# A two-layer recurrent block on one core: keys and queries of the first attention loaded in the projection's tail, one barrier less at each seam, and two engines' round loops written out

## The chip, the cores and the metric

One Trainium2 chip, of whose cores the kernel uses one. The program is written engine by engine: TensorE (PE, and PEld for its weight loads), VectorE (DVE), ScalarE (ACT), GpSimd (POOL) and SyncE (SP) each have a stream of instructions, and they meet only through semaphores. The metric is the time of one execution in device microseconds; the median over several executions is compared.

## The reference

Two layers. Each normalises x, computes an attention s and a feed-forward value g, and adds s * g to x. Only what the kernel does differently per layer matters here:

```python
x = L0_attn_x                                  # [2, 2048, 256], 16 heads of 16
xn = layernorm(x)
s = L0_attn(xn)                                # full softmax attention over 2048 keys
g = silu(L0_ffn(xn))                           # 8 experts, router softmax, cumulative sum over time
x = x + s * g
xn = layernorm(x)
s = L1_attn(xn)                                # banded attention: |i - j| <= 64
g = silu(L1_ffn(xn))                           # 8 LoRA experts, gate softmax
x = x + s * g
return x

# the first attention
qkv = einsum('bld,ed->ble', x, w_qkv) + b_qkv
attn = softmax(einsum('blhc,bmhc->bhlm', q, k) / sqrt(256))
heads = einsum('bhlm,bmhc->blhc', attn, v).reshape(b, l, d)
return einsum('bld,ed->ble', heads, w_o) + b_o + x
```

## The kernel before

Seven phases follow each other, with their starts in the profile: `phase_weights` (0 us), `phase_project` for layer 0 (44), `phase_attend_full` (213), `phase_combine_experts` (1660), `phase_project` for layer 1 (1971), `phase_attend_band` (2069) and `phase_combine_lora` (2331 to the end). Each opens one `nc.Block` with a program for each engine. A block ends with a barrier of all engines. Each phase takes its tiles and semaphores through an object `Names`; when the phase is over, `Names.release` (L85 to L89) clears the semaphores and has a second barrier of all engines. Buffers that several phases share belong to outer `Names` objects (tags k0 to k3), which release the same way, so at the first attention's start two such barriers stand behind the block's own.

`phase_project` walks over 4 chunks of 512 tokens (i) of 2 batches (u). For each chunk, TensorE makes queries, keys, values and the router's hidden layer, VectorE and ScalarE move them out of PSUM, and SyncE stores them to DRAM: `store_parts` (L476, 4 DMAs of 512 KB: queries and keys, each value split in a high and a low half) and `store_values` (L482, one of 544 KB). SyncE's last steps are the waits for all these stores (L532 to L538). Each DMA of SyncE goes onto one ring, in the order of its program. `load_rows`, `store_xn` and `store_turned` stand on it too. GpSimd computes inverse roots for the layernorm.

`phase_attend_full` works in NIT = 32 rounds: 8 groups of 4 heads, 4 chunks of 512 queries in each. The four heads lie in two slots and two sides of 64 partitions; a side holds three copies of 16 rows, for the high and low halves. Per round there are two passes:

- the maximum pass, NU = 32 units: `maximum_scores` (L1147, two matmuls of 128 queries by 512 keys), then `maximum` on VectorE (L1026) over 1024 columns. `whole_maxima` (L1034) closes it. The maxima are turned by TensorE, split into two halves by VectorE (`split_maxima`), and written by GpSimd as extra rows of the query tile Q (`store_maxima`, L984, 4 small DMAs), where the second score matmul subtracts them.
- the exponential pass, NJ = 43 steps: `scores` (L1173), `exponential` on ScalarE (L1091, up to 1024 columns into the ring `prob`), and `add_values` (L1185), which multiplies with the values V and accumulates in PSUM. `copy_output` (L1098), the turn back and `normalise` give `o_out`, which GpSimd stores (`store_output`, L990).

The passes are interleaved: while round r is exponentiated, the maxima of round r + 1 are taken. Before the first round there is a prologue of 32 units without exponentials. In it TensorE also turns eight weight tiles (`turn_weights`, L1240), in units 1 to 8. Ahead of all that, VectorE clears `ps_o` (L1059) and runs the router's softmax (`router_weights_vector`, L1815 to L1831) with ScalarE's exponential (L1805) between L1817 and L1819.

What the first units need comes by DMA at the start of the phase. SyncE issues 12 key loads of slot 0 and slot 1 (`load_first_keys`, L818, 128 KB each into 16 partitions), 18 query loads (`load_first_queries`, L827, 64 KB each), then four loads of V (`load_v`, L944), then, when all keys and queries have landed, the 30 loads of group 1 (`load_halves`, L795 and L799). ScalarE issues the six loads of the first queries itself, and four loads of rows of ones. TensorE waits for them at L1247 to L1256. GpSimd's program ends with a wait for all output stores (`pool.wait_ge(o_stored, ...)`); in `phase_attend_band` SyncE ends with such a wait.

The rounds of TensorE, VectorE, ScalarE and GpSimd are loops (`Fori`) over two rounds each; VectorE's loop spans rounds 0 to 29, ScalarE's rounds 1 to 30, while round 0 of ScalarE is written out.

## Time and profile before

| | us |
|---|---|
| median of 3 runs | 2436.63 |
| lowest and highest | 2425.33, 2439.51 |
| profiled execution | 2435.27 |
| its span | 2433.4 |
| mean granted TensorE clock | 0.956 |
| share of the span busy: PE, DVE, ACT | 91%, 76%, 59% |

The runs are whole executions; the profiled one is a single execution, and its span runs from the first instruction to the last. All rows below have their times in microseconds from the start of that span. A row of the timeline gives start, duration, engine, source line, operation and tiles; "SPq" and the like is an engine's instruction queue, where semaphore and DMA-issuing instructions stand. The landing time of a DMA is counted from its issue. "PEclk" is the granted clock as a share of full speed, "DMA" the mean busy share of the 16 DMA engines. In the view of busy time by stretch the columns are the stretch, its length, the busy time (and number of instructions) of PE, PEld, DVE, ACT and POOL, PEclk, the DMA share, and GB/s.

### The profile page before, as it was taken

What the parts mean: (1) busy time and instruction counts of PE and PEld (TensorE: products, weight loads), DVE (VectorE), ACT (ScalarE), POOL (GpSimd) and SP (SyncE); (2) the same over time, 40 slices, a digit from 0 to 9 for tenths busy, and PEclk for the clock granted to TensorE, in tenths of its full rate; (3) what the DMA queues carried; (4) which work ended last, traced back from release to release, by engine and by line L of the source; (5) the groups of instructions that cost most, each with busy time, mean ns of one, the idle gap of its engine ahead of it and who ended that gap; (6) DMA issues with size and microseconds to landing.
All of it is one profiled execution on the core that took longest, in us unless ns stands there. A gap on an engine that the chain in (4) does not pass through costs nothing. (4 is left out here: it accounts for less than half of the span.)

```text
span 2433.4 us, 43647 instructions
## 1 busy us (share of the span) xinstructions
PE 2212.6 (91%) x14912; PEld 1228.7 (50%) x14912; DVE 1839.2 (76%) x3240; ACT 1442.7 (59%) x2160; POOL 462.6 (19%) x673
## 2 busy tenths in 40 slices
PE   7896899999999999999999999988999987899988
PEld 4664333333333333333333333326888876666678
DVE  5664999999999999999999999912444466888745
ACT  3443377777777777777777777772222222366743
POOL 0000000000000000000000000003545520366745
PEclk9997699999999999999999999989999999688999
DMA  6888400500500501403205002006576459766664
GB/s 206 283 288 183 53 6 6 62 6 8 62 3 13 57 3 26 44 6 44 26 3 64 6 8 62 3 3 176 154 186 157 135 190 373 170 145 146 154 164 130
DMA packets 189129, 231.90 MB, mean 95 GB/s; under 512 B 72720, under 2 KB 122768, under 8 KB 186064
## 3 DMA queue, kind: packets, MB, share of 16 engines
q1 hardware_dynamic: 176048, 210.46, 35.3%
q10 hardware_dynamic: 7184, 14.10, 2.7%
q0 software_dynamic: 5728, 5.00, 0.9%
q8 instruction: 117, 1.92, 0.4%
q14 instruction: 52, 0.43, 0.1%
HBM read 138.97 MB, written 89.13 MB: 94 GB/s over the span
## 5 line engine op out<-in xcount | busy, mean ns | idle before, releaser
L1026 DVE TENSOR_REDUCE a_maxes<-a_ps_a 128x2 f32<-128x1024 f32 x1024 | 1202.2, 1221 | 114.3 <-PE a_ps_a L1147 110.5
L1091 ACT ACTIVATE a_prob<-a_ps_s 128x512 f32<-128x512 f32 (+1 forms) x1376 | 1035.7, 804 | 355.2 <-PE a_ps_s L1173 349.5
L1173 PE MATMUL a_ps_s<-a_Q,a_K 50*128 50x512 f32 x2048 | 596.3, 455 | 89.8 <-ACT a_prob L1091 89.6
L1147 PE MATMUL a_ps_a<-a_K,a_Q 48*128 48x512 f32 x2048 | 551.9, 455 | 26.0 <-DMA a_Q<-s_halves 14.4
L1185 PE MATMUL a_ps_o<-a_prob,a_V 128*17 128x512 f32 x4096 | 544.9, 604 | 0.1
L1173 PEld LDWEIGHTS a_ps_s<-a_Q,a_K 50*128 50x128 f32 x2048 | 278.4, 186 | 508.7 <-ACT a_prob L1091 459.7
L1147 PEld LDWEIGHTS a_ps_a<-a_K,a_Q 48*128 48x128 f32 x2048 | 245.8, 189 | 231.5 <-issue 107.9
L984 POOL DMA_DIRECT2D a_Q<-a_m_parts x128 | 64.3, 503 | 1286.9 <-DVE a_m_parts L1018 1280.3
L1593 DVE CUSTOM_DVE_ANT_0 a_scratch<-a_ps_a,k_mask 128x256 f32<-128x256 f32 (+1 forms) x512 | 178.0, 411 | 25.9 <-PE a_ps_a L1710 24.0
L1653 ACT ACTIVATE a_prob<-a_ps_s 128x512 f32<-128x512 f32 (+1 forms) x256 | 135.6, 583 | 98.8 <-PE a_ps_s L1746 97.3
L1185 PEld LDWEIGHTS a_ps_o<-a_prob,a_V 128*17 128x17 f32 x4096 | 68.0, 95 | 150.9 <-issue 99.0
L1710 PE MATMUL a_ps_a<-k_K,k_Q 48*128 48x256 f32 (+1 forms) x512 | 120.4, 359 | 16.3 <-PEq L89 11.5
L1746 PE MATMUL a_ps_s<-k_Q,k_K 50*128 50x256 f32 (+2 forms) x576 | 105.8, 314 | 12.6 <-DMA k_K<-k_ones 7.0
L1572 POOL TENSOR_SCALAR_AFFINE_SELECT a_prob<-a_prob 128x512 f32<-128x512 f32 (+1 forms) x128 | 79.5, 621 | 130.0 <-ACT a_prob L1653 129.0
L1746 PEld LDWEIGHTS a_ps_s<-k_Q,k_K 50*128 50x128 f32 x576 | 80.2, 203 | 42.3 <-ACT a_prob L1653 16.7
L2122 POOL TENSOR_TENSOR c_pT<-c_wp,c_pT 128x512 fp32r<-128x512 f32 x64 | 82.9, 1295 | 94.8 <-ACT c_pT L2045 94.8
L1710 PEld LDWEIGHTS a_ps_a<-k_K,k_Q 48*128 48x128 f32 x512 | 83.7, 217 | 27.6 <-issue 11.9
L2045 ACT ACTIVATE c_pT<-c_wp 128x512 fp32r<-128x512 f32 x64 | 40.5, 633 | 93.6 <-DVE c_wp L2086 89.6
L2019 PE MATMUL c_ps_g<-k_UO,c_pT 128*128 128x256 f32 x768 | 94.8, 280 | 0.0
L2019 PEld LDWEIGHTS c_ps_g<-k_UO,c_pT 128*128 128x128 f32 x768 | 92.9, 188 | 0.0
L2159 DVE TENSOR_TENSOR c_sums<-c_ps_s,c_sums 128x256 f32<-128x256 f32 x32 | 13.6, 424 | 90.2 <-ACT c_th L2056 90.2
L1575 POOL TENSOR_SCALAR_AFFINE_SELECT a_prob<-a_prob 128x512 f32<-128x512 f32 (+1 forms) x128 | 79.4, 621 | 0.0
(195 smaller groups left out, 2260.2 us busy)
## 6 DMA issues: line engine op xcount, KB each, us to landing
s_halves<-p_parts SPq DMA_DIRECT2D x32, 512.0 KB, 5.1
s_halves<-k_K SPq DMA_DIRECT2D x32, 512.0 KB, 7.7
a_Q<-s_halves SPq DMA_DIRECT2D x186, 64.0 KB, 10.5
a_K<-s_halves SPq DMA_DIRECT2D x42, 256.0 KB, 9.0
s_xT<-p_xT SPq DMA_DIRECT2D x32, 256.0 KB, 4.0
s_cT<-p_cT SPq DMA_DIRECT2D x32, 256.0 KB, 3.7
k_wb<-s_w SPq DMA_DIRECT2D x16, 512.0 KB, 7.7
c_wb<-s_w SPq DMA_DIRECT2D x16, 512.0 KB, 8.1
```

Source lines behind the costliest of these rows:

```text
L1026: nc.vector.tensor_reduce(maxes[:, :, slot, qt, kc], ps_a[:, o:o + 2 * CH].rearrange("p (z k) -> p z k", z=2), AX.X, ALU.max).then_inc(a_d ...
L1091: nc.scalar.activation(prob[:, ring:ring + len(t), :].rearrange("p r q -> p (r q)"), ps_s[:, bank:bank + len(t) * CH], ACT.Exp, scale=scal ...
L1147: last = nc.tensor.matmul(ps_a[:, o + side * CH:o + (side + 1) * CH], Q[rows, q0:q0 + P], K[rows, k0:k0 + CH], start=True, stop=True)
L1173: last = nc.tensor.matmul(ps_s[:, bank + x * CH:bank + (x + 1) * CH], K[rows, k0:k0 + P], Q[rows, q0:q0 + CH], start=True, stop=True)
L1185: last = nc.tensor.matmul(ps_o[h * VW:h * VW + VC, :], V[:, kt, h * VC:(h + 1) * VC], prob[:, ring, :], start=(kt == 0), stop=(kt == KT - ...
L1572: pool.affine_select(out=left, in_=left, compare_op=ALU.is_ge, fill=0.0, base=first, pattern=[[0, G], [1, P - first]], channel_multiplier= ...
L1593: nc.vector.tensor_tensor_reduce(scratch[:, (2 * a + x) % (2 * BANKS), first:last], ps_a[:, o + first:o + last], W["mask"][:, first:last], ...
L1653: nc.scalar.activation(prob[:, s % RING, side, :, first:last], scores[:, :, first:last], ACT.Exp, scale=scale).then_inc(exp_done, 1)
L1710: last_mm = nc.tensor.matmul(ps_a[:, o + first:o + last], Q[rows, query(g, slot, (qt0 + x) * P):][:, 0:P], K[rows, base + lo:base + hi], s ...
L1746: last_mm = nc.tensor.matmul(ps_s[:, c0:c0 + q1 - q0], K[rows, k0:k0 + P], Q[rows, query(g, slot, q0):][:, 0:q1 - q0], start=True, stop=Tr ...
L2019: last = nc.tensor.matmul(g_region(t), pT[:, s, ft, t * P:(t + 1) * P], W["UO"][:, m, ft, :], start=False, stop=(ft == FT - 1 and s == 1), ...
L2122: pool.tensor_tensor(pT[:, 1, ft, :], wp[:, ft % 2, :], f32(pT[:, 0, ft, :]), ALU.subtract).then_inc(p_low, 1)
```

## The change

1. Barriers. Seven phases, and the new object for the shared attention buffers, hand their semaphores to a list `W["retired"]` on release, without clearing them and without a barrier. `clear_retired` clears the list on GpSimd at the end of the next phase's program, and once at the very end. The objects k1, k2 and k3 keep their clearing and barrier.
2. Early loads. K and the space of V are allocated before the first projection (`attention_buffers`). The projection's xT lies in the second half of K, the first queries go to `Q_first` in the space of V. In the projection's last step (i = 3, u = 1) SyncE loads the keys of slot 0 before `store_parts`, and the first queries and the keys of slot 1 after it, ahead of `store_values`. TensorE's prologue reads `Q_first`.
3. The attention's start. SyncE loads all 24 query tiles into Q, waits until the prologue's 32 units are done (since V's space holds `Q_first`), and then loads V. ScalarE does the router's exponential first and the rows of ones after it. VectorE does the first part of the router (L1815, L1817), four units, the second part (L1819 to L1831), then the other 28 units. The weight turns move from units 1 to 8 to units 6 to 13.
4. Waits for stored outputs. `o_out` and `o_stored` now belong to buffers that outlive the phase; the waits move to SyncE in the following phases, before the loads for a later chunk.
5. Loops. VectorE's and ScalarE's loops over the rounds are Python loops now, so their instructions are written out.

```diff
 def release(self):
-        if self.sems:
+        if self.retired is not None:
+            self.retired.extend(self.sems)
+        elif self.sems:
             self.nc.clear_and_free_semaphores(self.sems)
             self.nc.all_engine_barrier()
...
+def clear_retired(nc, W):
+    if W["retired"]:
+        nc.clear_and_free_semaphores(W["retired"])
+        W["retired"].clear()
...
+def attention_buffers(n):
+    half = PAIR * T
+    K = n.sb("K", [P, 2 * half], F32R, side="right")
+    VQ = n.sb("VQ", [P, KT * G * VC], F32R, side="right")
+    return {"K": K, "V": f32(VQ[:]).rearrange("p (t n) -> p t n", t=KT), "Q_first": VQ[:, 0:PAIR * CH],
+            "own_xT": K[:, half:2 * half].rearrange("p (u a k t) -> p u a k t", u=2, a=2, k=DK),
+            "k_first": [n.sem(f"k_first{slot}") for slot in range(PAIR)], "q_first": n.sem("q_first")}
...
@@ phase_project, SyncE @@
+                    if first and not more and u == 1:
+                        for m in range(4):
+                            wait_apart(sp, parts_stored[m], DMA * 2 * NCH, passed)
+                        load_first_keys(sp, A["K"], S, 0, A["k_first"][0])
                     store_parts(sp, i, u)
+                    if first and not more and u == 1:
+                        load_first_queries(sp, A["Q_first"], S, 0, A["q_first"])
+                        load_first_keys(sp, A["K"], S, 1, A["k_first"][1])
                     if after:
                         store_turned(sp, *after)
                     if not more and u == 1:
                         second_halves(sp, 0)
                     store_values(sp, i, u)
...
@@ phase_attend_full, SyncE @@
-            for slot in range(PAIR):
-                load_first_keys(sp, K, S, slot, k_first[slot])
-            for qc in range(1, NCH):
+            for qc in range(NCH):
                 load_first_queries(sp, Q, S, qc, kq_loaded)
-            sp.sem_inc(kq_loaded, (HALVES_LOADS - (NCH - 1) * FIRST_LOADS) * DMA)
+            sp.sem_inc(kq_loaded, (HALVES_LOADS - NCH * FIRST_LOADS) * DMA)
+            wait_apart(sp, a_done, 2 + NU, passed)
             for q in range(4):
                 load_v(sp, 0, q)
...
@@ GpSimd @@
-            pool.wait_ge(o_stored, DMA * (NIT + 2))
+            clear_retired(nc, W)
...
@@ VectorE @@
-            router_weights_vector(nc, dve, W, r_top, r_total, r_inv, router_step, router_exp)
-            dve.wait_ge(router_step, 7)
-            for k in range(NU):
-                maximum(0, k, bank_of(0, k))
+            for part in range(2):
+                router_weights_vector(nc, dve, W, r_top, r_total, r_inv, router_step, router_exp, part)
+                for k in range(*((0, SOFT_AT) if part == 0 else (SOFT_AT, NU))):
+                    maximum(0, k, bank_of(0, k))
...
-            with dve.Fori(0, NIT // 2 - 1) as i:
-                iteration(2 * i, 0, True)
-                iteration(2 * i + 1, 1, True)
+            for it in range(NIT - 2):
+                iteration(it, it % 2, True)
...
@@ ScalarE @@
-            load_first_queries(act, Q, S, 0, q_first)
+            act.sem_inc(exp_done, 2)
+            router_weights_scalar(nc, act, W, router_step, router_exp)
             for side in range(2):
                 for row in range(2):
                     r = side * SIDE + ROW_M0 + row
                     act.dma_start(f32(K[r:r + 1, :]), W["ones"][:, 0:2 * LONG // P]).then_inc(rows_set, DMA)
-            act.sem_inc(exp_done, 2)
-            router_weights_scalar(nc, act, W, router_step, router_exp)
...
-            with act.Fori(0, NIT // 2 - 1) as i:
-                for r in (1, 2):
-                    for j in range(NJ):
-                        exponential(2 * i + r, r % 2, j)
-                        if j == COPY_AT:
-                            copy_output(2 * i + r - 1)
...
+            for it in range(1, NIT):
+                for j in range(NJ):
+                    exponential(it, it % 2, j)
+                    if j == COPY_AT:
+                        copy_output(it - 1)
...
@@ TensorE, prologue @@
-                maximum_scores(0, 0, k, bank_of(0, k))
-                if 0 < k <= len(w_turns):
-                    turn_weights(k - 1)
+                maximum_scores(0, 0, k, bank_of(0, k), Q_first)
+                if SOFT_AT + 2 <= k < SOFT_AT + 2 + len(w_turns):
+                    turn_weights(k - SOFT_AT - 2)
...
@@ phase_combine_experts, SyncE @@
+                    if c == 1:
+                        wait_apart(sp, X["o_stored"], DMA * (NIT + 2), passed)
                     load_attention(c)
...
@@ phase_combine_lora, SyncE @@
+                    if c == 0:
+                        for b in range(2):
+                            wait_apart(sp, KQ["o_stored"][b], DMA * NCH * NG // 2, passed)
                     load_attention(c + BUFS)
```

## Rows read from the trace of the kernel before

**Rows 1.** Busy time of each engine by stretch, one steady round

```profile
1000.00:1042.67 42.67, 39.98 (x265) 15.71 (x266) 38.90 (x38) 32.92 (x45) 2.77 (x6) 1.00 0.02 4
```

**Rows 2.** One line's instructions: L1034, ns min/median/max, first and last start

```profile
L1034 DVE TENSOR_REDUCE a_neg_max<-a_maxes x32: 219/220/222, 266.9 to 1590.6; 128x16 f32<-128x64 f32 x32
```

**Rows 3.** The same view of L1117, ScalarE's loop, 460 to 1560 us

```profile
L1117 ACTq COMPARE_BRANCH  x13: 45/45/45, 492.8 to 1516.9; - x13
```

**Rows 4.** Timeline of ScalarE in rounds 0 and 1: start, us, instructions

```profile
307.85 2.00 ACT L1091 ACTIVATE a_prob<-a_ps_s 128x512 f32<-128x512 f32 x3 [0.37 <-PE a_ps_s L1173]
...
315.99 2.00 ACT L1091 ACTIVATE a_prob<-a_ps_s 128x512 f32<-128x512 f32 x3 [0.36 <-PE a_ps_s L1173]
...
350.52 2.00 ACT L1091 ACTIVATE a_prob<-a_ps_s 128x512 f32<-128x512 f32 x3 [0.37 <-PE a_ps_s L1173]
...
358.65 2.00 ACT L1091 ACTIVATE a_prob<-a_ps_s 128x512 f32<-128x512 f32 x3 [0.36 <-PE a_ps_s L1173]
```

**Rows 5.** Timeline of SyncE's DMA issues, 205 to 230 us

```profile
208.58 0.37 SPq L482 DMA_DIRECT2D s_v<-p_v_out  x1
213.26 6.21 SPq L818 DMA_DIRECT2D a_K<-s_halves  x12
```

**Rows 6.** Waits, 213 to 227 us: us in total, times, longest

```profile
PE a_ps_a L1147 <- DMA a_Q<-s_halves: 14.0, 1, 14.0
```

**Rows 7.** Timeline of VectorE, 211 to 240 us

```profile
214.50 0.69 DVE L1817 TENSOR_TENSOR k_logits<-k_logits,a_prob 128x512 f32<-128x512 f32 x1
220.79 0.69 DVE L1819 TENSOR_REDUCE a_prob<-k_logits 128x64 f32<-128x512 f32 x1 [5.59 <-ACT k_logits L1805]
...
222.63 0.69 DVE L1831 TENSOR_TENSOR k_logits<-k_logits,a_prob 128x512 f32<-128x512 f32 x1
...
226.76 3.49 DVE L1026 TENSOR_REDUCE a_maxes<-a_ps_a 128x2 f32<-128x1024 f32 x3 [3.44 <-PE a_ps_a L1147]
...
232.26 1.23 DVE L1026 TENSOR_REDUCE a_maxes<-a_ps_a 128x2 f32<-128x1024 f32 x1 [0.47 <-PE a_ps_a L1147]
233.96 1.23 DVE L1026 TENSOR_REDUCE a_maxes<-a_ps_a 128x2 f32<-128x1024 f32 x1 [0.47 <-PE a_ps_a L1147]
```

**Rows 8.** Busy time by stretch, around the seam (columns of rows 1)

```profile
194.10:208.90 14.80, 14.61 (x76) 10.92 (x76) 4.71 (x10) 5.48 (x8) 0.00 (x0) 1.00 0.38 143
213.20:225.50 12.30, 0.02 (x2) 0.02 (x2) 4.11 (x8) 2.43 (x3) 1.28 (x2) 0.55 1.01 131
225.50:241.00 15.50, 15.10 (x54) 6.07 (x54) 11.08 (x10) 4.69 (x8) 0.00 (x0) 0.50 1.04 123
```

**Rows 9.** Barriers and waits at the seams, by line (SPq L60: view of waits)

```profile
L386 SPq EVENT_SEMAPHORE  x1: 17/17/17, 212.1 to 212.1; - x1
...
L89 SPq EVENT_SEMAPHORE  x2: 17/17/17, 212.8 to 213.2; - x2
...
L893 POOLq DRAIN  x1: 3495/3495/3495, 1655.7 to 1655.7; - x1
...
SPq L60 <- DMA s_att<-a_o_out: 1.5, 1, 1.5
...
L1453 SPq EVENT_SEMAPHORE  x1: 17/17/17, 2330.5 to 2330.5; - x1
...
L89 SPq EVENT_SEMAPHORE  x1: 17/17/17, 2331.3 to 2331.3; - x1
```

**Rows 10.** DMA issues (KB, us to landing) around 220; instruction queue, 460 to 1660

```profile
s_v<-p_v_out SPq DMA_DIRECT2D x1, 544.0 KB, 3.0
...
a_K<-s_halves SPq DMA_DIRECT2D x12, 128.0 KB, 10.3
...
s_att<-a_o_out POOLq DMA_DIRECT2D x1, 128.0 KB, 8.6
...
q8 instruction: 57, 0.93, 0.4%
...
a_Q<-a_m_parts POOLq DMA_DIRECT2D x108, 4.0 KB, 1.6
```

More of the change, by code:

```diff
@@ L386, in phase_project @@
     with ExitStack() as ctx:
-        n = Names(nc, ctx, f"p{layer}")
+        n = Names(nc, ctx, f"p{layer}", W["retired"])
         xn = L["xn"]
-        xT = n.sb("xT", [P, 2, 2, DK, CH], F32R) if first else KQ["own_xT"]
+        xT = A["own_xT"] if first else KQ["own_xT"]
         cum = n.sb("cum", [P, DK, CH]) if first else None
@@ L392, in phase_project @@
         cT = n.sb("cT", [P, 2, 2, DK, CH], F32R) if first else None
-        parts = n.sb("parts", [P, 4, 2, CH], F32R) if first else KQ["parts"]
+        if first:
+            parts = [A["xT"][:, 0], A["xT"][:, 1], A["cT"][:, 0], A["cT"][:, 1]]
+        else:
+            parts = [KQ["parts"][:, m] for m in range(4)]
         v_out = n.sb("v_out", [P, 2, NG2, TT, G * VC]) if first else KQ["v_out"]
@@ L476, in store_parts @@
                 sp.dma_start(S["halves"][m // 2, u, :, (m % 2) * P:(m % 2 + 1) * P, tok]
[L477 removed]
+                             .rearrange("a p t -> p a t"), f32(parts[m])).then_inc(parts_stored[m], DMA)
         def store_values(sp, i, u):
@@ L914, in phase_attend_full @@
         kq_loaded = n.sem("kq_loaded")
-        k_first = [n.sem(f"k_first{slot}") for slot in range(PAIR)]
-        q_first = n.sem("q_first")
         router_step = n.sem("router_step")
@@ L1146, in maximum_scores @@
                     k0 = half + slot * T + kc * CH
-                    last = nc.tensor.matmul(ps_a[:, o + side * CH:o + (side + 1) * CH], Q[rows, q0:q0 + P],
+                    last = nc.tensor.matmul(ps_a[:, o + side * CH:o + (side + 1) * CH], queries[rows, q0:q0 + P],
                                             K[rows, k0:k0 + CH], start=True, stop=True)
@@ L1487, in phase_attend_band @@
         o_clear = n.sem("o_clear")
-        o_stored = [n.sem(f"o_stored{b}") for b in range(2)]
+        o_stored = KQ["o_stored"]
         block = ctx.enter_context(nc.Block())
@@ L1561, in _ @@
             store_output(NCH * NG - 1)
-            for b in range(2):
-                wait_apart(sp, o_stored[b], DMA * NCH * NG // 2, passed)
         @block.gpsimd
```

88 lines of the change are left out of this document (47 added, 41 removed).

## The prediction

> **What bounds the kernel now.** I read the slices of the page first: TensorE is busy for nine tenths nearly everywhere, with a dip of the granted clock near the start. So the question is whether a change touches the 32 rounds of the first attention, or only the seams between the phases. A steady round of 42.67 us has TensorE busy 39.98, VectorE 38.90 and ScalarE 32.92 [rows 1], and the 32 row maxima that end a round's maximum pass run from 266.9 to 1590.6 us [rows 2], 42.7 us apart. The rounds are 1366 of the 2433.4 us of the span. They are set by TensorE and by its exchange of tiles with ScalarE, not by any seam. The loop's own cost is the next thing to look at: ScalarE closes its loop with a branch of 45 ns [rows 3]. Round 0 of ScalarE is written out, round 1 is already in the loop, and the timeline shows the same exponentials at the same pace in both: 307.85 to 315.99, 8.14 us, in round 0; 350.52 to 358.65, 8.13 us, in round 1 [rows 4].
>
> Then the seams. The worst is the one from the first projection to the first attention. SyncE issues the last store (values) at 208.58; the first keys only at 213.26 [rows 5]; TensorE stands 14.0 us waiting for the queries' DMA [rows 6]; VectorE's first maximum starts at 226.76 [rows 7]. Meanwhile the DMA engines were only 0.38 busy in the projection's tail (194.1 to 208.9) and full from 213.2 on, at 131 GB/s [rows 8]. That idle share is what the change means to use.
>
> **The change, part by part.** All sums are against the profiled execution of before, 2435.27 us; the median of the runs shown is 2436.63, 1.4 above it.
>
> *The early loads.* Without any delay, the phase's barriers would end one barrier earlier: 0.6 us, from the two barriers at 212.8 and 213.2 after the block's at 212.1 [rows 9]. The clearing of PSUM and the first half of the router stay ahead of VectorE's first maximum; they ended at 214.50 + 0.69 = 215.2 [rows 7]. The keys being there, the first maximum would start at about 215.2 - 0.6 + 0.2 (the handover) = 214.8 instead of 226.76: 12.0 us gained.
>
> But the loads stand on SyncE's ring ahead of the store of the values, and the phase ends with a wait for that store. SyncE is free for the first six key loads at about 192; the four stores of parts follow at 195.6 to 200.6, then six query and six more key loads at 0.36 us of issue each, over by 205.1. So the store's issue at 208.58 is not delayed; its data are. The added bytes are 12 x 128 KB + 6 x 64 KB = 1.97 MB (the key row of [rows 10]; each lands in 16 partitions). At the 131 GB/s of [rows 8] this takes 15.0 us of full engines, at the 123 GB/s of the next stretch 16.0. The tail of 14.8 us has 0.62 x 14.8 = 9.2 us free [rows 8]. The store's data thus start 5.8 us late (15.0 - 9.2), 6.8 at 123 GB/s, 8.1 if queries in rows of 2 KB run still slower (114 GB/s). I take 6.8. The store itself takes 3.0 us from issue to landing [rows 10], as before. Behind that wait stand the barrier and everything of the attention: the loss counts in full. The bounds are 0 (the narrow key rows cost the wide store nothing) and 8.1.
>
> The narrow rows' rate stands in the trace: 131 GB/s, against some 380 in the stores from all partitions. The Trainium skill, "SBUF — State Buffer", section "Door 1: The DMA port swizzle (why [64,N] ≈ [32,N])", says that a DMA is as fast as the number of ports that its partitions reach, at 27.2 GB/s each; by its table 16 partitions in a row reach four. Estimated from that page, 1.97 MB take 18.1 us, and the result would be 3.1 us worse than by the row, some 2431.
>
> *The router.* Its second half now stands between VectorE's units 4 and 5 instead of before the first, where it was hidden by the wait for the queries. It runs from 220.79 to 222.63 + 0.69: 2.5 us [rows 7], on the engine that sets the pace of these units (spaced 233.96 - 232.26 = 1.70 us with a weight turn, [rows 7]). I take all of it, 2.6 with its waits. Cover could come only where TensorE is behind: the units with turns take 1.70 us against 1.23 of maximum [rows 7], and a TensorE that runs ahead during the pause could give that back. Bounds 0 and 2.6. The eight weight turns move from units 1 to 8 to units 6 to 13, at the same price.
>
> *Values and next keys later.* The V loads now wait for the whole first maximum pass, about 261 us, and the 30 loads of the next group stand behind them. SyncE has nothing else to do. Values are wanted some 12 us later, four times what a store of the same size took to land (3.0, [rows 10]). But the group's loads now run beside POOL's first four maxima rows. These land in 1.6 us, the median over all rounds [rows 10], and in before they were there 2.8 us ahead of TensorE's first scores by the timeline; the one output store that POOL issued beside full engines took 8.6 [rows 10]. Bounds: 0 and 8.6 - 1.6 - 2.8 = 4.2. Maxima rows are 4 KB against that store's 128, and every fourth round's run near group loads, so I take 0.5.
>
> Together at this seam: 12.0 - 6.8 - 2.6 - 0.5 = 2.1 us gained (all good bounds 12.0, all bad 12.0 - 8.1 - 2.6 - 4.2 = -2.9).
>
> *The other seams.* Each loses one barrier. At 0.6 us for one [rows 9] the seams weights to projection, attention to combination and combination to projection give 0.55 + 0.6 + 0.6; projection to band attention half of it, 0.25, because its first loads wait for stores anyway; the very end 0.3. The wait for the stored output goes to a later phase. After the first attention POOL's drain takes 3.5 us [rows 9] from the end of that wait; it would start earlier by up to 1.8, and I take 0.9. After the band attention SyncE's wait for that landing took 1.5 us [rows 9], and the barrier there 0.85 (2330.5 to 2331.3, [rows 9]): 2.4. In the next phase both waits find stores that landed long before; what stands behind them on SyncE are loads for the second chunk, so they cost nothing. Clearing the semaphores is now POOL's work at the end of its program in the next phase, where it ends early. Sum 2.3 + 0.9 + 2.4 = 5.6, bounds 3.5 and 7.
>
> *Loops written out.* By [rows 4] 0. Thirty rounds without a gain each; the bounds are below, as rivals.
>
> Sum: 2.1 + 5.6 = 7.7 us, so 2427.6 for a profiled execution; with the 1.4 between it and the median, rounded down, **2428.5** (0.3% faster).
>
> **Rivals.** *The tail takes the loads free (0.15).* The store of the values isn't held up: 6.8 more, 2421.7. For it: the tail ends in some 6 us without any DMA. Against it: 15 us of full engines don't fit in 9.2.
>
> *The clock stays up in the first units (0.1).* TensorE's granted clock was 1.00 to the tail's end and 0.50 in the units [rows 8], after it had stood idle. With the pause cut from 14 to some 10 or fewer us it could stay. Then the eight units with turns (1.70 against 1.23) save 8 x 0.47 = 3.8. The first round's exponentials, beside a TensorE at half clock until 289.5 us, could give as much again: about 7 more, 2421. Against it: units bound by VectorE leave TensorE half idle even at the full clock.
>
> *Slower: written-out streams wait for their instructions (0.08).* The instruction queue of TensorE moved 57 packets, 0.93 MB, over 1200 us of rounds, and took 0.4% of 16 engines: 0.004 x 16 x 1200 / 57 = 1.35 us for a packet of 16 KB [rows 10]. TensorE's 265 matmuls and 266 loads of a round [rows 1] are thus 33 KB, 62 bytes each. ScalarE's 45 and VectorE's 38 instructions, doubled for their waits, come to 10 KB a round, which their loops now keep. If each of these packets was waited for, 0.64 x 1.35 = 0.86 us a round, 26 us in 30 rounds: 2454. The point from which it decides is 7.7 / 30 = 0.26 us a round. Against it: TensorE streams three times as much at no visible wait.
>
> *Faster rounds (0.05).* In the written-out round some exponentials began up to 0.08 us sooner after TensorE's scores than in the loop. If that came off each of the 20 waits of TensorE in a round, 1.6 x 30 = 48 us: 2380. Against it: [rows 4]. The Trainium skill, "Runtime: NRT & Kernel Launch", section "Instruction fetch mechanics", says that a taken branch out of the two pages at hand stalls the engine, so by it writing loops out should gain at every back edge. The trace shows a branch of 45 ns and no later exponential.
>
> *The maxima rows land late (0.06):* 4.2 - 0.5 = 3.7 less, 2432.2. My forecast itself: 0.56, its own range 2424 to 2434.
>
> **How the numbers follow.** Under 2417 lie the faster rounds and a rest; over 2439 most of the slower rival: 0.13 outside plus some of the noise of runs (2425.33 to 2439.51 for one kernel), so 2417 to 2439 holds 8 in 10. About 1% is what a measurement of this kernel can tell: under 2412 only the faster rounds, 0.05; over 2461 only the slower rival at its upper end, 0.03; else 0.92.
>
> **What would show it.** Right: VectorE's first maximum near 221.6 us (214.8: the tail was free; 226 or later: the loads cost what they gain); the value store landing near 218 instead of 211.6; a pause of 2.5 us on VectorE after unit 4; POOL's maxima rows landing in 2 us; 32 row maxima still 42.7 apart; granted clock 0.5 in the first units. Wrong: any other spacing of the row maxima, since 0.26 us there outweighs all seams, or instruction packets of ScalarE or VectorE with idle time next to them.

## The result and the profile after

| | before | changed |
|---|---|---|
| median | 2438.77 us (10 runs, 2425.21 to 2443.81) | 2417.27 us (10 runs, 2411.29 to 2429.79) |
| profiled execution, span | 2433.4 | 2412.6 |
| mean granted clock | 0.956 | 0.957 |

The ratio is 0.992, with a 95% interval of 0.990 to 0.994: 21.5 us by the medians, 20.8 by the profiled executions. The forecast was 7.7 us.

The tail of the projection and the prologue, by the busy time in stretches (columns: stretch, length, PE, PEld, DVE, ACT, POOL, clock, DMA share, GB/s), the timeline of SyncE's DMA issues and of VectorE:

```profile
194.10:208.90 14.80, 13.78 (x72) 10.12 (x72) 3.96 (x9) 5.63 (x9) 0.00 (x0) 1.00 1.00 261
205.00:209.00 4.00, 2.90 (x18) 1.17 (x16) 0.76 (x2) 1.42 (x3) 0.00 (x0) 1.00 0.95 201
215.00:225.00 10.00, 5.85 (x18) 2.28 (x19) 9.56 (x13) 1.22 (x2) 0.00 (x0) 0.50 1.05 142
```

```profile
190.75 3.05 SPq L839 DMA_DIRECT2D k_K<-s_halves  x6
...
206.97 0.40 SPq L495 DMA_DIRECT2D s_v<-p_v_out  x1
212.23 11.81 SPq L848 DMA_DIRECT2D a_Q<-s_halves  x24
```

```profile
214.08 4.61 DVE L1053 TENSOR_REDUCE a_maxes<-a_ps_a 128x2 f32<-128x1024 f32 x4
218.61 0.68 DVE L1841 TENSOR_REDUCE a_prob<-k_logits 128x64 f32<-128x512 f32 x1
...
221.05 3.48 DVE L1053 TENSOR_REDUCE a_maxes<-a_ps_a 128x2 f32<-128x1024 f32 x3
...
226.54 1.23 DVE L1053 TENSOR_REDUCE a_maxes<-a_ps_a 128x2 f32<-128x1024 f32 x1 [0.47 <-PE a_ps_a L1167]
```

The first maximum is at 214.08 instead of 226.76 [rows 7]. The DMA engines are full in the tail instead of 0.38 busy [rows 8]: over the projection's last 25 us (186.0 to 211.2 us, before 187.6 to 211.6, each to the store's landing) their share is 0.98 instead of 0.56, which makes 24.7 us of full engines instead of 13.4. VectorE's pause for the second half of the router is there (218.61 to 221.05), and so is the low clock of the first units (0.50). SyncE's issue of the values' store did not move because of the new loads, as forecast (206.97; all of the projection is some 1.6 us earlier). It lands 4.2 us after its issue, against 3.0 in [rows 10]:

```profile
s_v<-p_v_out SPq DMA_DIRECT2D x1, 544.0 KB, 4.2
...
a_Q<-a_m_parts POOLq DMA_DIRECT2D x4, 4.0 KB, 7.4
```

These are issues and their landings, 205 to 209 us and 258 to 263 us. In the ten executions of this document that have the loads ahead of the store, it landed after 4.2 to 5.5 us; the first figure is the lowest of them. The second row is GpSimd's first four maxima rows, 1.6 us before. TensorE waits for them (the view of waits, 257 to 272 us):

```profile
PE a_ps_s L1193 <- DMA a_Q<-a_m_parts: 3.4, 1, 3.4
```

The 32 row maxima, and GpSimd at the end of the attention, by line:

```profile
L1061 DVE TENSOR_REDUCE a_neg_max<-a_maxes x32: 219/220/221, 257.2 to 1577.8; 128x16 f32<-128x64 f32 x32
```

```profile
L66 POOLq DRAIN  x1: 882/882/882, 1638.8 to 1638.8; - x1
...
L924 POOLq DRAIN  x1: 51/51/51, 1639.9 to 1639.9; - x1
L924 SPq EVENT_SEMAPHORE  x1: 17/17/17, 1640.2 to 1640.2; - x1
```

Where [rows 2] span 1323.7 us, these span 1320.6. The first interval grew from 43.6 to 45.4 us (the wait above is in it), the others shrank from 42.67 to 42.50. And GpSimd's drain (DRAIN, which each engine executes ahead of a barrier, and GpSimd ahead of a clearing too) of 3.5 us [rows 9] is gone.

How far each point of the program moved against before, in the two profiled executions (below zero is earlier):

| at | us |
|---|---|
| the projection's end | -1.6 |
| the first maximum | -12.7 |
| row maximum 1 | -9.7 |
| row maximum 2 | -7.8 |
| row maximum 32 | -12.8 |
| the attention's last output | -14.3 |
| the first work of the combination | -19.8 |
| the combination's end | -20.6 |
| the second projection's end | -20.8 |
| the band attention's end | -18.2 |
| the end | -20.8 |

### The profile page after: what moved, and what is told of

Its sections match the earlier page's. It is cut to its first block and busy times, and to the rows that moved or that the text cites. A ratio compares the mean times of both kernels' runs of the same rounds, so it can differ in the third digit from the quotient of the medians.

```text
span 2412.6 us, 41274 instructions
## 1 busy us (share of the span) xinstructions
PE 2208.1 (92%) x14912; PEld 1223.4 (51%) x14912; DVE 1840.9 (76%) x3240; ACT 1442.4 (60%) x2160; POOL 463.5 (19%) x673
## 5 line engine op out<-in xcount | busy, mean ns | idle before, releaser
L1117 ACT ACTIVATE a_prob<-a_ps_s 128x512 f32<-128x512 f32 (+1 forms) x1376 | 1035.7, 804 | 344.9 <-PE a_ps_s L1193 323.5
L1193 PE MATMUL a_ps_s<-a_Q,k_K 50*128 50x512 f32 x2048 | 593.6, 452 | 90.0 <-ACT a_prob L1117 85.3
L1205 PE MATMUL a_ps_o<-a_prob,k_VQ 128*17 128x512 f32 x4096 | 543.2, 602 | 0.1
L1193 PEld LDWEIGHTS a_ps_s<-a_Q,k_K 50*128 50x128 f32 x2048 | 275.7, 185 | 509.8 <-ACT a_prob L1117 455.9
L1167 PE MATMUL a_ps_a<-k_K,a_Q 48*128 48x512 f32 x1984 | 525.9, 444 | 3.9 <-DVE a_maxes L1053 3.5
L1167 PEld LDWEIGHTS a_ps_a<-k_K,a_Q 48*128 48x128 f32 x1984 | 232.4, 186 | 196.6 <-issue 105.0
L1205 PEld LDWEIGHTS a_ps_o<-a_prob,k_VQ 128*17 128x17 f32 x4096 | 67.9, 95 | 150.3 <-issue 102.8
L1766 PE MATMUL a_ps_s<-k_Q,k_K 50*128 50x256 f32 (+2 forms) x576 | 107.4, 318 | 12.8 <-DMA k_K<-k_ones 7.5
```

What stands on the lines that cost most here:

```text
L1117: nc.scalar.activation(prob[:, ring:ring + len(t), :].rearrange("p r q -> p (r q)"), ps_s[:, bank:bank + len(t) * CH], ACT.Exp, scale=scal ...
L1167: last = nc.tensor.matmul(ps_a[:, o + side * CH:o + (side + 1) * CH], queries[rows, q0:q0 + P], K[rows, k0:k0 + CH], start=True, stop=True)
L1193: last = nc.tensor.matmul(ps_s[:, bank + x * CH:bank + (x + 1) * CH], K[rows, k0:k0 + P], Q[rows, q0:q0 + CH], start=True, stop=True)
L1205: last = nc.tensor.matmul(ps_o[h * VW:h * VW + VC, :], V[:, kt, h * VC:(h + 1) * VC], prob[:, ring, :], start=(kt == 0), stop=(kt == KT - ...
L1766: last_mm = nc.tensor.matmul(ps_s[:, c0:c0 + q1 - q0], K[rows, k0:k0 + P], Q[rows, query(g, slot, q0):][:, 0:q1 - q0], start=True, stop=Tr ...
```

## The experiments

All experiments are cut from the changed kernel where nothing else is said. A single profile is compared by its timeline and by the distance of its row maxima, and not by its time, because that moves by some 30 us with TensorE's clock (the last experiments show this). From the second distance on, the distances repeat to 0.04 us where nothing disturbs them. The first distance does not: the changed kernel gave 45.4 us in one execution and 50.0 in another, since the clock was low until 278 us in the one and until 291 us in the other.

**Which engine's loop made the rounds shorter.** e1_act_loop puts ScalarE's loop back, e2_dve_loop VectorE's.

```diff
-            for it in range(1, NIT):
-                for j in range(NJ):
-                    exponential(it, it % 2, j)
-                    if j == COPY_AT:
-                        copy_output(it - 1)
+            with act.Fori(0, NIT // 2 - 1) as i:
+                for r in (1, 2):
+                    for j in range(NJ):
+                        exponential(2 * i + r, r % 2, j)
+                        if j == COPY_AT:
+                            copy_output(2 * i + r - 1)
...
-            for it in range(NIT - 2):
-                iteration(it, it % 2, True)
+            with dve.Fori(0, NIT // 2 - 1) as i:
+                iteration(2 * i, 0, True)
+                iteration(2 * i + 1, 1, True)
```

> The changed kernel with ScalarE's round loop put back; VectorE's rounds stay written out. In the changed kernel the 32 row maxima are 42.50 us apart against 42.67 before, and within a round the whole 0.17 us arises at two of ScalarE's exponentials, each 0.08 us sooner, where the loop had a second wait against a register's value. Theory (ScalarE's second waits are the cause): spacing back to 42.67, so 30 x 0.17 = 5.1 us longer. Rival (VectorE's written-out rounds are the cause, since it hands TensorE its banks): spacing stays at 42.50. Second rival (each engine gives a part): between, near 42.58.

> The changed kernel with VectorE's round loop put back; ScalarE's rounds stay written out. Theory (ScalarE alone): spacing of the row maxima stays at 42.50 us and the time at that of the changed kernel, about 2413 us. Rival (VectorE): 42.67, 5.1 us longer.

With VectorE's loop the row maxima stayed 42.49 to 42.54 us apart behind a first distance of 48.8. VectorE has no part in the gain of the rounds. The time was 2424.6 us, 12 more than expected. Of the 10 us over the changed kernel's profile 3.4 lie in the first distance and 5.2 in the last round, both with a clock that was low for longer (0.75 on average from 1590 to 1645 us). With ScalarE's loop, every other distance was 42.67 to 42.71 as in the theory, and from the fourth on the ones between were 44.4 to 52.5 us long, which nothing had foretold: 2483.9 us in all. Row maxima of e1_act_loop, by line; and ScalarE's loop, 640 to 680 us:

```profile
L1061 DVE TENSOR_REDUCE a_neg_max<-a_maxes x32: 219/220/221, 256.2 to 1637.2; 128x16 f32<-128x64 f32 x32
```

```profile
L1142 ACTq COMPARE_BRANCH  x1: 45/45/45, 668.8 to 668.8; - x1
L1142 ACTq FUSED_REGOPS  x1: 68/68/68, 671.4 to 671.4; - x1
```

Behind the same branch of 45 ns as in [rows 3] the loop's next register instruction comes 2.6 us later (before, 0.25), and over all passes 2.4 to 2.7. And the instruction queue q14, which between 460 and 1560 us moved nothing before and 28 packets of 8 KB in the changed kernel, moved 69:

```profile
q8 instruction: 51, 0.84, 0.4%
q14 instruction: 69, 0.57, 0.2%
```

Queue q14 is not ScalarE's alone. Where only ScalarE's rounds are written out it moves 19 packets (e2_dve_loop), where only VectorE's are, 10 (e7_act_loop_pad16, below). So of the 69 some 59 are ScalarE's, about five for each of some 12 passes of the loop, and four came between 668 and 676 us, right behind the branch.

**Why the same loop costs 50 us in one place and nothing in another.** The loop's body is 266 instructions in both kernels. Its start lies 10 instructions earlier in e1_act_loop (313 records of ScalarE ahead of it against 323). Two kernels shift it with idle increments of a spare semaphore ahead of round 0. e7_act_loop_pad16 is e1_act_loop with 16, e8_before_pad118 the kernel before with 118.

```diff
+            for _ in range(16):            # 118 in the kernel before
+                act.sem_inc(pad, 1)
             for j in range(NJ):
                 exponential(0, 0, j)
```

> e1_act_loop (the changed kernel with ScalarE's round loop, 2484 us, every second round 1.7 to 9.8 us longer, 123 instruction packets of 8 KB for ScalarE against 46 before) with 16 increments of a spare semaphore put on ScalarE's queue ahead of round 0, where it is idle. The loop's body is 266 instructions, and its start lies 10 instructions earlier than in the kernel before. Theory (whether the loop stays in the instruction buffer depends on where its body lies against the blocks of 8 KB, at 62 bytes each some 130 instructions, in which they are fetched; 10 earlier takes it over a border): with 16 more it lies as before, all rounds take 42.68 us, and the time is 2413 + 5 = 2418 us, 65 less. Rival (the stalls come from what else changed: other loads or other engines' streams): every second round stays longer and the time near 2484.

> The mirror of e7_act_loop_pad16: the kernel before, with 118 increments of a spare semaphore on ScalarE's queue ahead of round 0, where it is idle for 37 us. They shift the loop by 118 instructions, which is 10 back from its old place, modulo 128. Theory (the loop's place in the 8 KB blocks decides): every second round takes 1.7 us or more longer, the instruction packets of ScalarE rise from 46 to over 100, and the kernel takes 2480 us or more. Rival: 42.67 us for every round and 2436 us.

Both came as the theory said. With 16 instructions more, all distances behind the first were 42.62 to 42.69 us. The last row maximum was 5.1 us later than in the changed kernel, as expected, though the whole took 2423.7 us instead of 2418. The loop then begins 6 instructions behind its old place, so more than one place is free. With 118 more, every second distance of the kernel before grew to 44.4 to 50.2, and it took 2491.2. Row maxima and instruction queues, 460 to 1560 us, first of e7_act_loop_pad16, then of e8_before_pad118:

```profile
L1062 DVE TENSOR_REDUCE a_neg_max<-a_maxes x32: 219/220/222, 258.0 to 1582.8; 128x16 f32<-128x64 f32 x32
...
q14 instruction: 10, 0.08, 0.0%
```

```profile
L1035 DVE TENSOR_REDUCE a_neg_max<-a_maxes x32: 219/221/222, 266.4 to 1650.4; 128x16 f32<-128x64 f32 x32
...
q14 instruction: 60, 0.49, 0.1%
```

So the loop of the kernel before had a lucky place: with a body of a little more than two packets of 8 KB (266 instructions at the 62 bytes that the prediction found), nothing is fetched on a pass, or some five packets are on each, by where it begins. That it stays in a buffer in the one case is inferred from the packets. The written-out stream of ScalarE is fetched too, 17 packets in the 1100 us of e11_before_open_inc, one every 65 us on average, and no distance of row maxima shows a wait for it. (By the pages of the profiles, the packets of e1_act_loop and before over the whole span are 130 and 52, not the 123 and 46 of the expectations.)

**Where the 0.17 us of a round come from.** In the kernel before and in the changed one, the same stretch of a round (ScalarE's timeline; the number in brackets is the idle time; the last line takes in one exponential more in the second):

```profile
1004.68 1.09 ACT L1091 ACTIVATE a_prob<-a_ps_s 128x512 f32<-128x512 f32 x2 [0.54 <-PE a_ps_s L1173]
1006.52 2.64 ACT L1091 ACTIVATE a_prob<-a_ps_s 128x1024 f32<-128x1024 f32 x3 [0.76 <-PE a_ps_s L1173]
...
1011.66 2.00 ACT L1091 ACTIVATE a_prob<-a_ps_s 128x512 f32<-128x512 f32 x3 [0.37 <-PE a_ps_s L1173]
1014.59 1.51 ACT L1091 ACTIVATE a_prob<-a_ps_s 128x1024 f32<-128x1024 f32 x2 [0.92 <-PE a_ps_s L1173]
```

```profile
994.06 1.08 ACT L1117 ACTIVATE a_prob<-a_ps_s 128x512 f32<-128x512 f32 x2 [0.61 <-PE a_ps_s L1193]
995.83 2.64 ACT L1117 ACTIVATE a_prob<-a_ps_s 128x1024 f32<-128x1024 f32 x3 [0.68 <-PE a_ps_s L1193]
...
1000.97 2.00 ACT L1117 ACTIVATE a_prob<-a_ps_s 128x512 f32<-128x512 f32 x3 [0.38 <-PE a_ps_s L1193]
1003.80 2.64 ACT L1117 ACTIVATE a_prob<-a_ps_s 128x1024 f32<-128x1024 f32 x3 [0.83 <-PE a_ps_s L1193]
```

The idle time is 0.76 and 0.92 us in the loop, 0.68 and 0.83 written out. Each exponential has two waits in the program. In the loop, ScalarE does arithmetic on a register for some of the second ones, 16 times in the round from 1000 to 1042.67 us (lines L1086 and L1088). Nine times another exponential is running meanwhile. Seven times ScalarE is idle and the exponential comes some 0.08 us later. At five of these the next exponential waits that much less for TensorE, and nothing is lost. At the other two, the arithmetic at 1006.4 and at 1014.5 us, nothing gives it back.

The piece that [rows 4] compares holds one such place too, in lines that are not shown there. Round 0, written out, then round 1, in the loop:

```profile
310.45 2.65 ACT L1091 ACTIVATE a_prob<-a_ps_s 128x1024 f32<-128x1024 f32 x3 [0.60 <-PE a_ps_s L1173]
314.12 1.51 ACT L1091 ACTIVATE a_prob<-a_ps_s 128x512 f32<-128x512 f32 x2 [1.02 <-PE a_ps_s L1173]
```

```profile
353.12 1.51 ACT L1091 ACTIVATE a_prob<-a_ps_s 128x1024 f32<-128x1024 f32 x2 [0.60 <-PE a_ps_s L1173]
354.82 1.02 ACT L1091 ACTIVATE a_prob<-a_ps_s 128x1024 f32<-128x1024 f32 x1 [0.19 <-PE a_ps_s L1173]
356.78 1.51 ACT L1091 ACTIVATE a_prob<-a_ps_s 128x512 f32<-128x512 f32 x2 [0.94 <-PE a_ps_s L1173]
```

Three exponentials take 2.65 us in the one and 1.51 + 0.19 + 1.02 = 2.72 in the other, and the next wait for TensorE is 0.94 instead of 1.02: the delay is there, and is absorbed.

Writing out ScalarE's rounds was tested alone, together with an independent edit at the attention's end, in e11_before_open_inc: the kernel before with ScalarE's rounds written out, and one instruction behind GpSimd's last wait.

```diff
             pool.wait_ge(o_stored, DMA * (NIT + 2))
+            pool.sem_inc(out_clear, 1)
```

> The kernel before with two independent edits: ScalarE's round loop written out (nothing else of the change), and on GpSimd one semaphore increment behind the final wait for the stored outputs. First: if ScalarE's second waits alone make the 0.17 us, the row maxima are 42.50 to 42.53 apart instead of 42.67, 5 us less in all; if the changed kernel's other edits are needed, 42.67 stays. Second, the drain of 3.5 us on GpSimd after that wait, which did not come back in e3_wait_back or e5_wait_last: if the branch that carried the wait makes it, the drain is now near 0.1 to 1 us and the seam takes 3 us less; if it is the first drain after the loop's DMAs, wherever the wait stands, 3.5 us stay. Together 2428 us for the one, 2431 for the other, against 2435.3 of the profiled execution of before.

The distances became 42.48 to 42.55: writing out ScalarE's rounds alone gives the whole 0.17 us. The ratio to the kernel before was 0.9954 (0.9924 to 0.9984), less than 1 by more than its uncertainty; 5.0 us of 2435 would be 0.998. GpSimd's drain stayed at 3.5 us. The profiled execution took 2434.4 us, neither the 2428 nor the 2431 expected: its first row maximum was 2.5 us later than before, and its last 2.2 us earlier.

**The seam behind the attention.** From VectorE's last instruction to the next phase's first it took 7.2 us before and 1.7 in the changed kernel. Three kernels take this apart: e3_wait_back has the wait for the stored outputs ahead of the clearing, e5_wait_last behind it, and e12_barriers_back has the clearing and the barrier back at all phases' ends.

```diff
+            pool.wait_ge(o_stored, DMA * (NIT + 2))      # e3
             clear_retired(nc, W)
+            pool.wait_ge(o_stored, DMA * (NIT + 2))      # e5
...
-        n = Names(nc, ctx, "a0", W["retired"])           # e12, and the same for w, p, c0, a1, c1
+        n = Names(nc, ctx, "a0")
```

> The changed kernel with GpSimd's wait for the stored outputs put back at the end of the first attention, ahead of its clearing of semaphores; the later wait stays too. Before, VectorE's last instruction ended at 1652.9 us and the next phase began at 1660.05, 7.2 us; in the changed kernel it is 1638.5 to 1640.2, 1.7 us: 5.5 gained, against 1.5 that I had forecast. Theory A (the wait and what it leads to, a drain of 3.5 us on GpSimd, cost nearly all of it): with the wait back the seam takes some 6.6 us again, the barrier's 0.6 apart. Theory B (the drain of 3.5 us comes from the wait being the last step, so that it becomes a branch out of the block): with the clearing behind the wait the drain is near 0.9 as in the changed kernel and only the landing, 1.7 us, comes back: seam 3.3 to 3.6 us.

> The changed kernel with GpSimd's wait for the stored outputs as the very last step of the first attention, behind its clearing of semaphores (in e3_wait_back it stood ahead of it, and the seam from VectorE's last instruction to the next phase's first took 3.3 us: only the landing came back, 1.7 us; the drain of 3.5 us of the kernel before did not). Theory B (a wait as the last step turns into a branch out of the block that carries the wait, and the drain behind it takes 3.5 us): the drain is back, and the seam takes 6.5 us or more, 3.2 over e3_wait_back. Rival (the 3.5 us belonged to something else in the kernel before, its outputs' buffer or the clearing behind the barrier): drain under 1 us, seam near 3.4 us.

> The changed kernel with each phase clearing its semaphores and meeting in a barrier again at its end; all else stays. Forecast of the term: 0.55 to 0.6 us at each of six seams and at the end, and less where a load is waited for anyway: 3.2 us over the changed kernel (0.25 of it at the second projection's end). Rival: clearing early on GpSimd gave nothing on the path, because other waits end last at the seams: under 1 us.

| | VectorE's last instruction ends | next phase begins | us |
|---|---|---|---|
| before | 1652.8 | 1660.05 | 7.2 |
| changed | 1638.5 | 1640.2 | 1.7 |
| e3_wait_back | 1634.0 | 1637.3 | 3.3 |
| e5_wait_last | 1636.8 | 1639.9 | 3.2 |
| e12_barriers_back | 1640.3 | 1645.9 | 5.5 |
| e11_before_open_inc | 1645.5 | 1652.6 | 7.1 |

The wait costs 1.5 to 1.6 us, the landing, wherever it stands. The rest comes with the clearing: where GpSimd clears semaphores at the end of its program, its drain takes 0.1 to 0.9 us and the block's own drain behind it 0.05. Where it doesn't, the block's drain is the first since the loop's DMAs and takes 3.5 us, whether the DMAs were waited for or not. In e12_barriers_back, by line:

```profile
L924 POOLq DRAIN  x1: 4278/4278/4278, 1640.6 to 1640.6; - x1
```

It begins beside the last store's issue (0.75 us) and ends 3.5 us behind it. Theory A of e3_wait_back, 6.6 us with the wait back, fell with the 3.3 measured. Theory B, a branch that carries the wait, fell twice: with the branch in e5_wait_last the drain was 0.05 us, and without it in e11_before_open_inc it was 3.5. Why the first drain is short when it belongs to a clearing stays open. At three seams where GpSimd had no such DMAs, e12_barriers_back took 0.5 to 0.7 us more than the changed kernel, as forecast for a barrier. At the second projection's end it took 1.2 more (VectorE idle 6.2 us against 5.0) where 0.25 was forecast, and at this seam 3.8 where 0.6 was; So the forecast of 3.2 us for all ends was too small, and so was its rival of under 1: added up over all ends the seams took some 8 of the 15.8 us that its profile has over the changed kernel's. Of the rest 1.3 are the values' store, which landed after 5.5 us instead of 4.2, and most is the clock: 3.7 more in the first distance of row maxima (49.1 us against 45.4), 6.6 more in the band attention, 5.2 less in the last round.

**The maxima rows.** e4_halves_late lets SyncE wait for the first maxima rows before it loads the second group.

```diff
             wait_apart(sp, kq_loaded, HALVES_LOADS * DMA, passed)
+            wait_apart(sp, m_loaded, 4 * DMA, passed)
             load_halves(sp, K, Q, S, kq_loaded, 1, 1)
```

> The changed kernel, but SyncE waits for the landing of the first four maxima rows before it issues the 30 loads of the second group. In the changed kernel these rows took 7.4 us to land beside those loads, and TensorE waited 3.4 us for them; before, they took 1.6 us. Theory: the landing goes back to 1.6 to 2.5 us, TensorE's wait is gone, and the second row maximum comes 2 to 3.4 us sooner (1.8 us were lost between the first and the second row maximum). Rival: the values' loads ahead of them are the cause, or GpSimd's own queue, and the landing stays above 5 us. Whole time 2 to 3 us below the changed kernel, if the clock comes back at the same point.

```profile
a_Q<-a_m_parts POOLq DMA_DIRECT2D x4, 4.0 KB, 1.6
```

That is the landing, 258 to 264 us. TensorE's wait for it is gone. It was 3.4 us in the changed kernel and 3.7 in its second profile (e10_changed_again, landing 7.3 us). The first distance of the row maxima fell from 45.4 to 42.1 us: 3.3 us, and 42.1 again in e9_late_spread, which has the same edit. The clock came back at 275.8 us instead of 278.2, and what of the 3.3 us is the wait itself and what the clock isn't separated. The whole profiled span was 2403.5, 9.1 less than the changed kernel's. 3.3 of them are this distance; 5.2 lie in the last round of the attention, where TensorE's clock fell in the one execution and not in the other (the busy time by stretch, first e4_halves_late, then the changed kernel, each to the attention's end):

```profile
1590.00:1628.00 38.00, 32.12 (x195) 9.47 (x191) 0.68 (x2) 30.81 (x42) 0.78 (x1) 1.00 0.02 5
```

```profile
1590.00:1635.00 45.00, 38.33 (x196) 10.51 (x196) 0.68 (x2) 32.69 (x44) 0.78 (x1) 0.85 0.02 4
```

**The tail's loads behind the store of the values**, e6_tail_late:

```diff
-  (six key loads ahead of store_parts, twelve loads behind it)
                     if not more and u == 1:
                         second_halves(sp, 0)
                     store_values(sp, i, u)
+                    (all eighteen loads here)
```

> The changed kernel with all 18 early loads issued behind the store of the values in the projection's tail, instead of ahead of it. The store then lands 3.0 us after its issue (4.2 in the changed kernel). Theory (narrow rows move at about 200 GB/s when their ring is alone, as in the changed kernel's tail from 205 to 209 us; my 131 GB/s was a mixture of two rings): keys of slot 0 and first queries, 1.2 MB, are there some 6 us after 208.5, so the first maximum comes at about 215, one us later than the 214.1 of the changed kernel, and the keys of slot 1 aren't missed. Rival (131 GB/s holds and the tail only had more room): the first maximum comes at about 218 or later. In either case the whole time moves by under 5 us.

The store landed after 3.5 us instead of 3.0. The first maximum came at 220.6, so both numbers for it were misses, for a reason that the traces of before and after showed and I had overlooked: the phase ends only when SyncE has issued all 18 loads, at 217.2 us, and the barrier follows. The rate of the narrow loads, which this run was meant to tell, stands in the stretch where they had the ring nearly alone:

```profile
209.00:215.00 6.00, 0.43 (x4) 0.32 (x4) 0.29 (x2) 0.00 (x0) 0.00 (x0) 0.69 1.06 160
```

It is 160 GB/s, between my two numbers. The first microsecond still holds the end of the values' store; from 210.3 to 217.2 us, without it, the view of the DMAs gives 152.

**A version beyond the change.** e9_late_spread is e4_halves_late with the weight turns in 16 units of two transposes.

```diff
-                if SOFT_AT + 2 <= k < SOFT_AT + 2 + len(w_turns):
-                    turn_weights(k - SOFT_AT - 2)
+                if SOFT_AT + 2 <= k < SOFT_AT + 2 + 2 * len(w_turns):
+                    turn_weights(*divmod(k - SOFT_AT - 2, 2))
```

> A version meant to beat both kernels: e4_halves_late (the second group's loads only after the landing of the first maxima rows) and, in the prologue, the 32 transposes of the router's weights in 16 units of two instead of 8 units of four. A unit with four takes 1.70 us where VectorE needs 1.23 (others 1.13 to 1.17), because TensorE at half clock is behind. Theory (TensorE has room for two transposes, some 0.28 us at half clock, in a unit): 8 x 0.55 = 4.4 us lost becomes 16 x 0 to 0.1, so the first row maximum comes 3 to 4 us earlier than in e4_halves_late (257.1), near 253.5, and the time is near 2402. Rival (the handover to ScalarE for each tile sets the 1.70, not TensorE's time): units stay at 1.4 and more, and nothing or up to 1 us is gained. Against the kernel before: 0.985 to 0.990.

> The changed kernel once more, on the same chip and in the same rounds as e9_late_spread, for a comparison of the two: 0.992 of the kernel before, as measured; e9_late_spread is expected 5 to 8 us below it.

In the timeline the edit does what it should. VectorE's 28 units behind the router now run without a gap:

```profile
216.88 4.61 DVE L1054 TENSOR_REDUCE a_maxes<-a_ps_a 128x2 f32<-128x1024 f32 x4
...
223.84 33.65 DVE L1054 TENSOR_REDUCE a_maxes<-a_ps_a 128x2 f32<-128x1024 f32 x28
```

From the first maximum to the first row maximum it takes 40.7 us, 2.5 less than the 43.1 of e4_halves_late and of the changed kernel; less than the 3 to 4 I had expected, and the first row maximum stood at 257.5 us, not at 253.5. The first maximum itself was 2.9 us later in this execution, and that lay in the first phases. The timed comparison can't tell the two versions apart: medians 2412.9 us (6 runs) and 2416.9 (7 runs of the changed kernel, 2409.1 to 2442.3), ratios to the kernel before 0.987 (0.982 to 0.992) for both. So a gain of 5.8 us, the sum of the two pieces, is not shown for the whole time. What hides it is the clock. The profiled execution of e10_changed_again has a span of 2440.6 us, 28 more than the first one of the same code, with the row maxima behind the first as evenly 42.50 apart. In its last round the clock stayed low nearly throughout:

```profile
1591.00:1646.00 55.00, 49.96 (x173) 12.49 (x173) 0.67 (x2) 29.20 (x39) 0.00 (x0) 0.51 0.00 0
```

## Why the prediction was right or wrong

The direction held, and so did the range (2417.3 in 2417 to 2439), but only by 0.3 us and by luck: the median of e10_changed_again, the same code, lies below it (2416.9). The size didn't hold: 7.7 us forecast, 20.8 found. Four terms were mis-sized, three of them the same way.

*The added loads, 6.8 us late.* Measured: the store landed 4.2 us after its issue instead of 3.0, 1.2 us late, and up to 2.5 late in the other executions, so the rival "the tail takes the loads free" was nearer to what happened than my term. The mechanism was right (same ring, ahead of the store) and the rate was wrong. I took 131 GB/s from the start of the attention [rows 8], where SyncE's and ScalarE's queues ran beside each other and many packets were of 2 KB. Over the whole tail they cost 24.7 - 13.4 = 11.3 us of full engines for the 1.97 MB, an estimate of 175 GB/s; from 205 to 209 us, with the start of the store, it was 201 GB/s, and 152 to 160 nearly alone in e6_tail_late. Against the 9.2 us free, 11.3 would make the store 2.1 us late, which is within the 1.2 to 2.5 measured. The bound of 8.1 put all bytes at the 114 GB/s that it names for the queries alone. The page "SBUF — State Buffer" of the Trainium skill, section "Door 1: The DMA port swizzle (why [64,N] ≈ [32,N])", gives four ports and some 109 GB/s for a DMA into 16 partitions. The trace goes beyond that, with 175 to 201 GB/s. The loads that follow each other in one queue go to different groups of partitions, which may be why; no run tests it. The first maximum came at 214.1, where I had given 214.8 for the case without delay, but the whole projection was 1.6 us earlier; on equal terms it was 0.9 later than that case.

*The router, 2.6 us.* Measured: 218.69 to 221.05, 2.4 us. The size was right, and nothing covered it. From the first maximum to the first row maximum it was 43.1 us instead of 40.1.

*The maxima rows, 0.5 us of a bound of 4.2.* Measured: landing 7.4 us, TensorE waiting 3.4, and the first distance was 3.3 shorter in e4_halves_late. The rival was the truth here too; the bound by the one row of that kind beside full engines (8.6 us, [rows 10]) was the better price than the median of 108 rows that mostly landed beside idle engines. Against before, whose clock stayed low for another length of time, it shows as 1.8 in the first distance.

*Seam by seam.* Measured from the block's last work to the next phase's first: weights to projection 0.54 (0.55 forecast), combination to projection 0.56 (0.6), to the band attention 0.29 by VectorE's idle time (0.25), band attention to combination 2.3 (2.4). At the attention's end it was 5.5 against 0.6 + 0.9: the landing gives 1.6 (e3_wait_back), and some 3.9 is the drain of 3.5 us with its barrier (e12_barriers_back). My step had the drain begin earlier. That it would all but vanish, because GpSimd's clearing now drains first, I had no row for, and I should have taken the upper bound as the whole 3.5 us of [rows 9].

*The loops, 0.* Measured: 42.67 to 42.50, 5.0 us in the rounds. The step that failed is the comparison of [rows 4]. It covers 8.1 us of a round, in which the one delay of the loop (354.82 us) is absorbed by the next wait for TensorE; the two places where it is not absorbed lie elsewhere. The rival "faster rounds" had the mechanism and the size of one event (0.08 us) but put it on 20 waits instead of 2. A look at the whole round of before would have shown the places; what they cost, only a written-out round to compare. The Trainium skill, "Runtime: NRT & Kernel Launch", section "Instruction fetch mechanics", has the rule that a branch out of the pages at hand stalls the engine. The traces agree where the loop lies badly (e1_act_loop, e8_before_pad118: 2.4 to 2.7 us behind the branch on every pass); the loop of before was just not such a case.

The rival of stalled written-out streams did not come, and neither did the clock that stays up: 0.50 from the first units on. Sum of what was found: 0.5 for the first barrier and some 1.1 of variation in the first phases, 11.1 to the first maximum, 3.0 and 1.8 lost up to the second row maximum, 5.0 in the rounds, 1.5 in the last round (clock), 5.5 at the seam, 0.8 in the next start: 20.7. Some 2.6 of these are variation (1.1) and clock (1.5), not the change. The later seams' 3.2 us were mostly taken back by the clock around the start of the band attention, which was at 0.50 for 58 us (from 2039) instead of 48 (from 2061). That this is chance and not the change, one execution of each can't show.

## What to carry to other kernels

When a change shifts code, a hardware loop can go from free to 50 us without an edit of its own: look at the instruction queue's packets during the loop, and pad or write the loop out. A queue can carry the packets of two engines. Price a small transfer beside a big one by the row where it ran beside a big one, not by the median of quiet ones. And compare rounds over their whole length: a gain of 0.4% sat in two of 43 steps, outside the piece that I had compared, where the same delay was absorbed by the next wait.

## What the runs showed of the hardware

- A loop of 266 instructions on ScalarE is free or costs 1.7 to 9.8 us on every pass, by where it starts (e1_act_loop against e7_act_loop_pad16, before against e8_before_pad118). 16 idle instructions ahead of it made a kernel 60 us faster.
- GpSimd's first drain after its DMAs takes 3.5 us at a block's end, although all of them had landed in the kernel before. As part of a clearing of semaphores the first drain takes 0.1 to 0.9 us, and the block's own behind it 0.05. Why is open.
- TensorE's clock is the main noise of this kernel. In the last round, which has no maximum pass, it fell to 0.50 in some executions and not in others: not before 1630 us in e4_halves_late, for 54.6 us in e10_changed_again. The profiled spans of the same code were 2412.6 and 2440.6 us, further apart than the change's own gain.
